# Two 3x3 convolutions whose halo operand holds a second, column-shifted copy of the halo rows: nine matmuls an image in place of twelve

## The chip, the cores and the metric

The kernel runs on one core of one Trainium2 chip. The metric is the device time of one execution in microseconds (us); the figure of a kernel is the median of its runs.

## What is computed

The input x has 8 images of 16 channels, 64 by 64 pixels. Four blocks follow one another, and each adds its result to x:

```python
x = x + L0(gn(x))   # a lattice of 16 cells, each a 3x3 convolution with bias and ReLU
x = x + L1(gn(x))   # one 3x3 convolution with circular borders, written in the reference with FFTs
x = x + L2(gn(x))   # a KAN convolution: 3x3 over SiLU and 8 spline features of each input
x = x + L3(gn(x))   # one 3x3 convolution with zero borders and a bias
```

gn is a group normalisation over 8 groups of channels of each image. Only L1 (the circular convolution) and L3 (the last convolution) are touched by the change.

## The kernel before

**Layout.** An image is held as 128 partitions by 16 wide rows of 33 columns (TS = 528 numbers, 512 of them pixels). The partition is (s, y, c): s is the parity of the column, y one of four interleaved row classes (row = 4q + y), c the channel. Each number is split into two parts, a rounded high part (written by ScalarE, ACT) and the remainder (written by VectorE, DVE), and a product of weight and image is three matmuls: high by high, high by low, low by high (`PRODUCTS`).

**One of the two convolutions, for one image** (`single_step`): all outputs need the rows of the own image at two column shifts (dx = 0 and 1: 2 x 3 matmuls of 128 x 128 by 512 columns). The outputs of row classes 0 and 3 also need the row class that lies in the next wide row above or below. Those rows are copied by DMA into a second operand, the halo: 64 rows (side, s, c), the other 64 rows of the operand being zero. It takes again two column shifts, 2 x 3 matmuls: twelve in all. The weights of the four cases stand in `W1` and `W3` as 4 tiles (own at two shifts, halo at two shifts) of two parts each; `single_spread` writes them by small DMAs from the POOL queue (24 for each convolution, in three steps of 8), and DVE clears rows 64 to 127 of the halo tiles of W1 at the start (`clear_weights`).

**Halo copies.** For L1, SP runs `l1_halos(j)` after all loads of the lattice: it waits until the low part of image j is there (`l1_lo`, line 778) and issues four DMAs from `circular_halos` (line 779). For L3, SP runs `l3_halos(b)` (lines 819 to 821): it waits for `l3_lo` and issues four DMAs from `image_halos`. TensorE (PE) waits in `l1_step` and `l3_step` for the low part and for all four DMAs of the image.

**The order around them.** In the last cell of the lattice PE runs, for b = 4 to 7, a cell step of 27 matmuls, small matmuls of means (`group_means`) and `l1_step(b - 4)`; then l1_step(4) to l1_step(7) follow, between them group means and `keep_warm` matmuls whose results nobody uses. Image j of L1 passes ACT (`l1_rows`), DVE (`l1_split_lo`), SP, the DMAs and PE in this order. The mean of image 3 for the KAN block (`group_means(1, 3)`) is queued on PE behind l1_step(5), and DVE's `tail(1, 3)` waits for it, with the whole of the first KAN features behind.

In the KAN block PE runs for each image b: 24 matmuls on the first four features (lines tagged 1696, as all of `products`), 30 matmuls of `halo_steps(b - 1)`, 6 on SiLU, from b = 3 the 12 of `l3_step(b - 3)`, and 24 on the other four features. SP runs for each image b: from b = 3 `l3_halos(b - 3)`, then 8 DMAs of the first features' halos (line 838; they wait until PE has read the halos of the image before), 4 for SiLU (line 835) and 8 for the other features. ACT may write the first features of the next image (line 1217) only after those 8 DMAs have landed; DVE writes their low part (line 1557), and PE's next image starts. After the last KAN image PE runs halo_steps(7), l3_step(5), group_means(2, 7), l3_step(6) and l3_step(7). The last image passes POOL (line 872), ACT (line 1229), DVE (line 1534), four halo DMAs (line 821), l3_step(7), DVE (line 1545) and the store.

## Time and profile before

| what | value |
|---|---|
| median of 3 runs | 1272.43 us (1270.22 to 1273.92) |
| span of the profiled execution, which is all that is known of its own time | 1275.4 us |
| mean granted TensorE clock over the span | 0.979 of full speed |
| busy share of PE, DVE, ACT, POOL | 93%, 60%, 53%, 30% |
| the lattice with L1's first images, to about | 1024 us |
| rest of L1 and the start of KAN, to about | 1098 us |
| KAN images 2 to 7 with L3's first images, to about | 1251 us |
| the last two images of L3 and the stores | to the end |

A time stamp is in us from the start of the span. The profile puts each wait down to the engine or DMA that released it. PE's clock has two levels here, 2.4 GHz (shown as 1.00) and 1.2 GHz (0.50); a mean between them is a stretch with both. An idle engine costs something only where the work that ends last waits for it.

### The profile page before, as it was taken

The numbers are of one execution on the slowest core, as the hardware profiler recorded it, in microseconds if no ns is written. First come the engines' busy times: TensorE is split into PE (matmuls) and PEld (weight loads), VectorE is DVE, ScalarE is ACT, GpSimd is POOL, SyncE is SP. The second block draws the span as 40 slices with busy tenths as digits, with TensorE's granted clock in tenths as the row PEclk, the third lists the DMA queues.
The fourth block names the chain that finished last, engine by engine and source line by source line (L and its number), as shares of the span: only waits on it lengthen the run. The fifth ranks groups of instructions, "written<-read, shape, count | busy, mean of one in ns | idle before, by whom it ended". The sixth has DMA issues, their size and how long they took to land.

```text
span 1275.4 us, 15041 instructions
## 1 busy us (share of the span) xinstructions
PE 1189.7 (93%) x5184; PEld 884.3 (69%) x5184; DVE 762.7 (60%) x967; ACT 675.0 (53%) x737; POOL 377.7 (30%) x544
## 2 busy tenths in 40 slices
PE   3888999999999999989999999998999987999995
PEld 2655677766666677766666677876777766777773
DVE  6798952455656522336554652226655789899952
ACT  1667854434544434444444543444434789789821
POOL 6221333235421012402113203633233542103212
PEclk9898999999999999999999999999999998999998
DMA  5899999999999967889989988988799414677773
GB/s 148 236 234 247 294 254 266 192 158 207 201 203 188 222 180 211 217 183 223 202 203 180 193 226 209 243 212 218 197 203 198 59 31 72 102 115 112 123 125 57
DMA packets 104687, 234.22 MB, mean 184 GB/s; under 512 B 36884, under 2 KB 49764, under 8 KB 96164
## 3 DMA queue, kind: packets, MB, share of 16 engines
q1 hardware_dynamic: 82624, 181.90, 66.1%
q0 software_dynamic: 15808, 24.31, 10.6%
q10 hardware_dynamic: 6180, 27.06, 6.7%
q8 instruction: 41, 0.67, 0.2%
q14 instruction: 34, 0.28, 0.1%
HBM read 124.15 MB, written 85.75 MB: 165 GB/s over the span
## 4 chain that ended last, share of the span: by engine, by line
PE 51%; SPq 19%; DVE 10%; DMA 10%; issue 5%; ACT 4%; POOL 0%; DVEq 0%; ACTq 0%; POOLq 0%
PE PB L1727 43%; SPq L807 15%; PE PB L1696 7%; DMA S<-lattice 4%; DMA lattice<-S 4%; SPq L786 2%; DMA F<-F 2%; ACT F L1141 2%; DVE S L1577 1%; DVE S L1564 1%; DVE S L1570 1%; DVE F L1557 1%; SPq L838 1%; PE PB L1687 1%; DVE F L1470 1%
## 5 line engine op out<-in xcount | busy, mean ns | idle before, releaser
L1727 PE MATMUL PB<-F,WA 128*96 128x512 f32 (+1 forms) x3792 | 916.9, 403 | 32.2 <-DVE F L1470 13.9
L1727 PEld LDWEIGHTS PB<-F,WA 128*96 128x96 f32 (+1 forms) x3792 | 662.7, 176 | 277.5 <-ACT F L1141 19.9
L1141 ACT ACTIVATE F<-S 128x2116 fp32r<-128x2116 f32 (+4 forms) x160 | 261.5, 1634 | 206.0 <-DMA S<-lattice 81.7
L1152 ACT ACTIVATE S<-PB,BIAS 96x512 f32<-96x512 f32 (+1 forms) x320 | 211.7, 683 | 294.5 <-PE PB L1727 292.3
L1458 DVE TENSOR_TENSOR F<-S,F 128x1089 fp32r<-128x1089 f32 (+2 forms) x80 | 121.4, 1518 | 184.2 <-ACT F L1141 183.3
L1460 DVE TENSOR_TENSOR F<-S,F 128x1058 fp32r<-128x1058 f32 x64 | 80.8, 1263 | 187.1 <-ACT F L1141 186.7
L1470 DVE CAST F<-F 64x528 fp32r<-64x528 f32 (+4 forms) x304 | 180.2, 642 | 3.5
L905 POOL DMA_DIRECT2D WA<-taps x76 | 56.5, 746 | 365.8 <-ACT S L1152 326.0
L1696 PE MATMUL PB<-F,WA 128*128 128x512 f32 x576 | 147.5, 414 | 14.0 <-DVE F L1557 14.0
L1696 PEld LDWEIGHTS PB<-F,WA 128*128 128x128 f32 x576 | 112.5, 197 | 43.3 <-issue 14.7
L1461 DVE TENSOR_TENSOR F<-S,F 64x1058 fp32r<-64x1058 f32 x64 | 82.1, 1282 | 0.0
L897 POOL DMA_DIRECT2D taps<-WX x112 | 68.2, 659 | 18.3 <-ACT S L1152 13.2
L872 POOL TENSOR_TENSOR RS<-VE,NHALF 128x1 f32<-128x1 f32 x25 | 27.9, 1115 | 121.0 <-DVE VE L1349 120.8
L890 POOL MEMSET WX<- 48x1600 f32 x18 | 26.3, 1461 | 108.8 <-ACT S L1152 84.4
L1464 DVE TENSOR_TENSOR F<-S,F 128x1089 fp32r<-128x1089 f32 x16 | 20.7, 1295 | 44.7 <-ACT F L1141 44.6
L1217 ACT ACTIVATE F<-S 128x2112 fp32r<-128x2112 f32 x16 | 31.4, 1964 | 23.3 <-DVE S L1577 12.2
L1190 ACT ACTIVATE S<-KS,CB 128x528 f32<-128x528 f32 x64 | 41.8, 725 | 0.2
L1557 DVE SCALAR_TENSOR_TENSOR F<-S,F 128x1056 fp32r<-128x1056 f32 x32 | 38.8, 1253 | 3.4 <-ACT F L1217 3.4
L1124 ACT ACTIVATE KAN<-X,NBI,RS 64x512 f32<-64x512 f32 (+1 forms) x48 | 32.5, 676 | 15.0 <-POOL F L1095 8.5
L1085 POOL DMA_DIRECT2D out<-OT x26 | 14.7, 574 | 83.1 <-DVE OT L1545 83.1
L1564 DVE SCALAR_TENSOR_TENSOR S<-S 128x2112 f32<-128x2112 f32 x16 | 37.7, 2354 | 2.3 <-ACT S L1201 2.3
L1577 DVE SCALAR_TENSOR_TENSOR S<-S 128x2112 f32<-128x2112 f32 x16 | 37.7, 2355 | 0.1
(130 smaller groups left out, 738.9 us busy)
## 6 DMA issues: line engine op xcount, KB each, us to landing
S<-lattice SPq DMA_DIRECT2D x448, 66.1 KB, 4.9
lattice<-S SPq DMA_DIRECT2D x32, 817.5 KB, 6.0
S<-lattice SPq DMA_DIRECT2D x160, 136.1 KB, 3.5
S<-lattice SPq DMA_DIRECT2D x72, 272.5 KB, 5.0
lattice<-S SPq DMA_DIRECT2D x52, 272.5 KB, 4.0
lattice<-S ACTq DMA_DIRECT2D x48, 272.5 KB, 4.7
lattice<-S ACTq DMA_DIRECT2D x16, 817.5 KB, 7.0
S<-lattice SPq DMA_DIRECT2D x160, 70.1 KB, 3.6
```

Source lines behind the costliest of these rows:

```text
L807: sp.dma_start(dst, src).then_inc(image_loaded[q], 16)
L897: pool.dma_start(dst, src).then_inc(tp_stored, 16)
L905: pool.dma_start(dst, src).then_inc(w_loaded[k % 2], 16)
L1141: act.activation(piece_view(s, h, 0), raw_view(s, h), ACT.Copy).then_inc(hi_ready, 1)
L1152: act.activation(wide(to[:, at:at + TS])[:, :, 0:RX], pixels(RING_BANK[n % SLOTS_O][0:cell.rows, :]), ACT.Relu, bias=BIAS[0:cell.rows, k:k ...
L1458: last = nc.vector.tensor_tensor(lo, raw, hi, ALU.subtract)
L1460: nc.vector.tensor_tensor(lo[:, 0:2], raw[:, 0:2], hi[:, 0:2], ALU.subtract)
L1461: last = nc.vector.tensor_tensor(lo[0:4 * C, 2:4], raw[0:4 * C, 2:4], hi[0:4 * C, 2:4], ALU.subtract)
L1470: last = nc.vector.tensor_copy(FP[4 * C:P, slot, part, to:to + n], FP[0:4 * C, slot, 0, source:source + n])
L1557: last = nc.vector.scalar_tensor_tensor(to[:, odd, :, 1], full[:, odd], 0.0, to[:, odd, :, 0].bitcast(F32), ALU.max, ALU.subtract)
L1696: last = nc.tensor.matmul(pixels(bank[:, :]), weights, moving, start=open_ and n == 0, stop=close and n == len(todo) - 1)
L1727: last = nc.tensor.matmul(bank, WA[0:rows, first:first + cell.rows], wide(FZ[0:rows, i % SLOTS_F, base:base + TS])[:, :, 0:RX], start=j == ...
```

## The change

`circular_halos` gets a parameter `shift`, and a new helper `shifted_halos` does the same for the last convolution: four further DMAs an image write the halo rows, moved by one column, into rows 64 to 127 of the halo operand. In L1 SP issues eight DMAs an image in place of four. In L3 SP issues eight for images 0 to 4; for images 5 to 7 SP issues four and ACT the four shifted ones, behind a new wait for `l3_lo(b + 1)` and ahead of the next image's `l3_rows`. The weights of the second halo shift go into rows 64 to 127 of halo tile 2 (`single_spread`: 32 DMAs for each convolution), tile 3 is no longer used, and the clear of W1's halo tiles goes. `single_step` does the halo with one shift, three matmuls for six. The waits of PE count eight DMAs an image.

```diff
--- before.py
+++ after.py
@@ -642,12 +642,18 @@
             for part in range(2):
                 src = WT[0:C, part, 0:720].bitcast(F32).rearrange("p (x f) -> p x f", x=5)
                 for s in range(2):
-                    blocks = [(s * 4 * C + y * C, 0, 4 - y) for y in range(4)]
-                    blocks += [(side * HALO + s * C, 2, (5, 0)[side]) for side in range(2)]
-                    for row, tile, first in blocks:
-                        dst = to[row:row + C, part, tile:tile + 2, :].bitcast(F32)
+                    for y in range(4):
+                        row, first = s * 4 * C + y * C, 4 - y
+                        dst = to[row:row + C, part, 0:2, :].bitcast(F32)
                         yield (dst.rearrange("p d (s f) -> p (d s) f", s=2),
                                src[:, s:s + 4, first * C:(first + 4) * C])
+                    for side in range(2):
+                        row, first = side * HALO + s * C, (5, 0)[side]
+                        for shift in range(2):
+                            dst = to[shift * 4 * C + row:shift * 4 * C + row + C, part, 2, :].bitcast(F32)
+                            x = s + 2 - 2 * shift
+                            yield (dst.rearrange("p (s f) -> p s f", s=2),
+                                   src[:, x:x + 2, first * C:(first + 4) * C])
 
         def own_tile(part, t, dx):
 
@@ -714,14 +720,27 @@
                 halo = halo_pair(g)[odd * 4 * C:(odd + 1) * 4 * C].rearrange("p t a f -> p (t a) f")
                 yield from image_halos(own, halo)
 
-        def circular_halos(z):
+        def circular_halos(z, shift):
 
             for side, y in enumerate((3, 0)):
                 for s in range(2):
                     rows = slice(s * 4 * C + y * C, s * 4 * C + (y + 1) * C)
-                    to = slice(side * HALO + s * C, side * HALO + (s + 1) * C)
-                    yield (F1[to, z, :, EXT:EXT + TS].bitcast(F32),
-                           F1[rows, z, :, 2 * RW * side:2 * RW * side + TS].bitcast(F32))
+                    first = shift * 4 * C + side * HALO + s * C
+                    at, n = 2 * RW * side + shift, TS - shift
+                    yield (F1[first:first + C, z, :, EXT:EXT + n].bitcast(F32),
+                           F1[rows, z, :, at:at + n].bitcast(F32))
+
+        def shifted_halos(own, halo):
+
+            for side, y in enumerate((3, 0)):
+                for s in range(2):
+                    src = own[s * 4 * C + y * C:s * 4 * C + (y + 1) * C].bitcast(F32)
+                    first = 4 * C + side * HALO + s * C
+                    dst = halo[first:first + C].bitcast(F32)
+                    if side == 0:
+                        yield dst[:, :, RW - 1:TS - 1], src[:, :, 0:TS - RW]
+                    else:
+                        yield dst[:, :, 0:TS - RW - 1], src[:, :, RW + 1:TS]
 
         def image_halos(own, halo):
 
@@ -775,8 +794,9 @@
 
                 z = j % SLOTS_1
                 sp.wait_ge(l1_lo, j + 1)
-                for dst, src in circular_halos(z):
-                    sp.dma_start(dst, src).then_inc(l1_halo[z], 16)
+                for shift in range(2):
+                    for dst, src in circular_halos(z, shift):
+                        sp.dma_start(dst, src).then_inc(l1_halo[z], 16)
 
             def store_outputs(s):
 
@@ -819,6 +839,9 @@
                 sp.wait_ge(l3_lo, b + 1)
                 for dst, src in image_halos(slot[:, 0], slot[:, 1]):
                     sp.dma_start(dst, src).then_inc(l3_halo[max(0, b - B + 3)], 16)
+                if b < B - 3:
+                    for dst, src in shifted_halos(slot[:, 0], slot[:, 1]):
+                        sp.dma_start(dst, src).then_inc(l3_halo[0], 16)
 
             for b in range(B):
                 if b >= 3:
@@ -1304,6 +1327,10 @@
                 if b == B - 2:
                     act.wait_ge(l3_clear, 2)
                 l3_rows(b)
+                slot = l3_slot(b)
+                act.wait_ge(l3_lo, b + 1)
+                for dst, src in shifted_halos(slot[:, 0], slot[:, 1]):
+                    act.dma_start(dst, src).then_inc(l3_halo[b - B + 3], 16)
 
 
         @block.vector
@@ -1319,7 +1346,6 @@
                 for first in (960, 2016, 2496, 2976):
                     nc.vector.memset(WA[4 * C:P, first:first + 96].bitcast(F32), 0.0)
                 nc.vector.memset(FZ[:, :, 2 * PIECE:FSLOT].bitcast(F32), 0.0)
-                nc.vector.memset(W1[4 * C:P, :, 2:4].bitcast(F32), 0.0)
                 nc.vector.memset(W3[:, :, :, :].bitcast(F32), 0.0).then_inc(wa_clear, 1)
 
             def turned_lo_part(name):
@@ -1733,15 +1759,13 @@
 
                 todo = [((weights[:, 0, 1 - dx], weights[:, 1, 1 - dx]), at_shift(own, P, dx)) for dx in range(2)]
                 products(bank, todo, True, False)
-                todo = [((weights[:, 0, 3 - dx], weights[:, 1, 3 - dx]), at_shift(halo, P, dx))
-                        for dx in range(2)]
-                return products(bank, todo, False, True)
+                return products(bank, [((weights[:, 0, 2], weights[:, 1, 2]), at_shift(halo, P, 0))], False, True)
 
             def l1_step(j):
 
                 z = j % SLOTS_1
                 pe.wait_ge(l1_lo, j + 1)
-                pe.wait_ge(l1_halo[z], 4 * 16 * (j // SLOTS_1 + 1))
+                pe.wait_ge(l1_halo[z], 8 * 16 * (j // SLOTS_1 + 1))
                 if j >= 2:
                     pe.wait_ge(added[1], j - 1)
                 single_step(OUT_BANK[j % 2], W1, F1_OWN[:, z], F1_HALO[:, z]).then_inc(l1_done, 1)
@@ -1813,7 +1837,7 @@
 
                 z = max(0, b - B + 3)
                 pe.wait_ge(l3_lo, b + 1)
-                pe.wait_ge(l3_halo[z], 4 * 16 * (b + 1 if z == 0 else 1))
+                pe.wait_ge(l3_halo[z], 8 * 16 * (b + 1 if z == 0 else 1))
                 if b >= 2:
                     pe.wait_ge(out_staged, b - 1)
                 single_step(LAST_BANK[b % 2], W3, l3_slot(b)[:, 0], l3_slot(b)[:, 1]).then_inc(l3_done, 1)
```

## Rows read from the trace of the kernel before

**Rows 1.** The page's chain that ended last: shares of the span by line

```profile
PE PB L1727 43%; SPq L807 15%; PE PB L1696 7%; DMA S<-lattice 4%; DMA lattice<-S 4%; SPq L786 2%; DMA F<-F 2%; ACT F L1141 2%; DVE S L1577 1%; DVE S L1564 1%; DVE S L1570 1%; DVE F L1557 1%; SPq L838 1%; PE PB L1687 1%; DVE F L1470 1%
```

**Rows 2.** Busy time by KAN image; columns: stretch, length, engines, clock, DMA share, GB/s

```profile
1171.05:1194.70 23.65, 23.21 (x99) 18.44 (x99) 23.37 (x23) 21.24 (x22) 6.68 (x6) 1.00 0.77 119
...
1218.35:1241.41 23.06, 23.06 (x98) 18.35 (x99) 11.83 (x18) 4.13 (x4) 3.00 (x6) 1.00 0.70 116
```

**Rows 3.** Groups by line and shape, PE; busy us, mean ns, idle before

```profile
L1696 PE MATMUL PB<-F,WX 128*128 128x512 f32 x96 | 26.1, 423 | 4.7 <-DMA F<-F 4.2 <-issue 0.5
...
L1696 PE MATMUL PB<-WA,W 128*128 128x512 f32 x72 | 18.0, 398 | 0.0
```

**Rows 4.** Chain of waits, 985 to 1100; columns: start us, us, what

```profile
991.98 5.91 DMA F<-F
...
998.02 3.09 PE PB L1696 x12
...
1025.66 0.58 SPq L779
...
1027.57 2.35 DMA F<-F
...
1030.17 4.49 PE PB L1696 x12
```

**Rows 5.** Timeline, 1034 to 1064; start us, us, engine, line, tiles, count, idle before

```profile
1034.98 0.16 DVE L1343 TENSOR_SCALAR GM<-PB 128x2 f32<-128x2 f32 x1 [1.59 <-PE PB L1647]
...
1062.90 8.60 PE L1696 MATMUL PB<-F,WA 128*128 128x512 f32 x24 [7.47 <-DVE F L1557]
```

**Rows 6.** Timeline of one KAN image, 1170 to 1205

```profile
1172.21 3.36 SPq L821 DMA_DIRECT2D WA<-WA  x4
...
1179.90 5.17 SPq L838 DMA_DIRECT2D F<-F  x8
...
1189.87 1.98 ACT L1217 ACTIVATE F<-S 128x2112 fp32r<-128x2112 f32 x1 [0.71 <-DMA F<-F]
...
1194.70 10.22 PE L1696 MATMUL PB<-F,WA 128*128 128x512 f32 x42 [0.44 <-DVE F L1557]
```

**Rows 7.** Timeline, the last images, 1245 to 1267

```profile
1245.79 3.03 PE L1696 MATMUL PB<-WX,WA 128*128 128x512 f32 x12
...
1248.65 2.99 PE L1696 MATMUL PB<-WA,W 128*128 128x512 f32 x12
...
1250.78 0.16 DVE L1337 SCALAR_TENSOR_TENSOR MV<-MV,NV 128x1 f32<-128x1 f32 x1
...
1251.49 0.28 PE L1647 MATMUL PB<-MV,G 128*128 128x2 f32 x2
...
1261.46 5.46 PE L1696 MATMUL PB<-F,W 128*128 128x512 f32 x12 [5.99 <-issue]
```

**Rows 8.** DMA engines: two short stretches, and issues of 1240.5 to 1241.25

```profile
990.00:992.00 2.00, 2.00 (x10) 1.57 (x9) 1.90 (x5) 1.99 (x3) 0.13 (x1) 1.00 1.09 59
...
1242.00:1244.00 2.00, 2.00 (x10) 1.60 (x9) 0.17 (x2) 0.00 (x0) 1.63 (x4) 1.00 1.09 149
...
WX<-F SPq DMA_DIRECT2D x2, 123.8 KB, 4.8
```

**Rows 9.** Start of the kernel, and the POOL queue at the weights of L3

```profile
21.75 0.48 DVE L1322 MEMSET WX<- 64x512 f32 x1
33.59 1.29 DVE L1458 TENSOR_TENSOR F<-S,F 64x1089 fp32r<-64x1089 f32 x1 [8.87 <-ACT F L1141]
...
L915 POOL DMA_DIRECT2D W<-WX x24: 514/514/682, 656.6 to 687.4; - x24
...
709.68 0.75 POOL L905 DMA_DIRECT2D WA<-taps  x1 [10.36 <-ACT S L1152]
```

**Rows 10.** Timeline of PE, two starts after idle time in the lattice

```profile
98.14 11.19 PE L1727 MATMUL PB<-F,WA 128*96 128x512 f32 x40 [1.82 <-ACT S L1152]
...
281.06 26.82 PE L1727 MATMUL PB<-F,WA 128*96 128x512 f32 x112 [1.10 <-ACT F L1141]
```


## The prediction

> **What bounds the kernel now.** The page's chain of waits comes first [rows 1]: most of what ends last is the lattice (its matmuls, line 1727, and SP's loads, line 807), which the change leaves alone. Products of line 1696, to which all 48 removed matmuls belong, hold 7%. So the question is not what 48 matmuls cost, but which of them end a wait. The groups by line give the price of one: 26.1 us for the 96 of L1 is 0.27 us, 18.0 us for 72 of L3 is 0.25 us (a mean duration of 400 ns overlaps the next one and is not the price) [rows 3]. If all 48 lay on the path, some 12 us would go.
>
> Three stretches decide. In L1 the chain runs through SP's halo DMAs: l1_step(0) starts when the fourth DMA has landed, and l1_step(5) too [rows 4]. What the reader is to see there is "DMA F<-F" right ahead of a matmul group: the operand is late, not PE. DVE in its turn sits idle for 1.59 us until the group means that PE has queued behind l1_step(5) [rows 5]. In the KAN block the busy times by image show PE at 23.21 and DVE at 23.37 of 23.65 us, so neither has much to give alone [rows 2]. The timeline shows a third loop of the same length: PE's halo steps free the halo tile, SP issues eight DMAs from 1179.90, ACT waits 0.71 us for their landing, and PE starts the next image at 1194.70 after an idle time of 0.44 us [rows 6]. From 1218.35 on PE alone fills the stretch, 23.06 of 23.06 us [rows 2], and from there to the end the last images pass from engine to engine [rows 7].
>
> **The sum** is made on the profiled execution, of which only the span of 1275.4 us is known; it is 3.0 us over the median of the runs, and I carry the difference over to the median, 1272.43.
>
> **L1, images 0 to 2.** The step between two of SP's issues is (1027.57 - 1025.66) / 3 = 0.64 us [rows 4], so four more end 2.55 us later. The eighth of image 0 would be issued at 991.98 + 2.55 = 994.5. How long it takes to land is not in the trace: 2.35 us as for image 5, or 5.91 us as for image 0 [rows 4], when the DMA engines were full (share 1.09 with only 59 GB/s [rows 8]). That is 996.9 to 1000.4. I take the middle, 998.7, since the load is on its way down by then: l1_step(0) starts 0.7 us later than its 998.02 (0 to +2.4). Nine matmuls for twelve give back 3 x 3.09 / 12 = 0.77 us in l1_step(0), (1) and (2), 2.3 us before image 5 is normalised behind the last cell. Halos 1 and 2 have a cell step of time and stay hidden; uncovered they would cost 2.55 us each. So image 5 is ready 1.6 us earlier (2.3 earlier to 0.1 later).
>
> **L1, image 5.** Its halo has no cover: +2.55 us. l1_step(5) starts at 1030.17 - 1.6 + 2.55 = 1031.1. Its 12 matmuls took 4.49 us, partly at half clock; after a longer idle time nine may all run at the 0.455 us of the last step (5.46 / 12 [rows 7]), 4.1 us. The saving is between 0.4 and 1.12 us (3/12 of 4.49); I take 0.4. Together **+0.55 us** at the wait of DVE [rows 5]. The good end is -2.3 + 2.55 - 1.12 = -0.9. At the bad end, 0.1 + 2.55 - 0.4 = +2.25, comes a clock that falls at l1_step(0): after 1.82 us idle 40 matmuls took 11.19 us, after 1.10 us idle 112 took 26.82 us, 0.280 against 0.239 us each, 1.6 us a fall [rows 10]; +3.9.
>
> **L1, image 7.** Its halo comes 2.55 us later too, hidden by PE's idle time of 7.47 us ahead of 1062.90 [rows 5]. 0; if that idle time got so short that the clock held, the 24 matmuls there could drop from 8.60 us towards 6.0: 0 to -2.6.
>
> **KAN images 3 to 6.** PE gets 0.75 us an image back, but the loops of DVE and of the halos stay, so its idle time grows from 0.44 to about 1.2 us and nothing ends sooner; DVE's own slack, 0.28 us an image, allows -1.1 in all. SP issues four more DMAs behind 1172.21: its 3.36 us become some 5.9, to 1178.1, ahead of 1179.90, when PE frees the tile [rows 6]. Hidden with 1.8 us to spare; without that cover the eight halo DMAs queued behind would start later, and ACT, DVE and PE with them. Traffic may still push their landing: 4 x 63 KB at 149 GB/s [rows 8] is 1.7 us of the DMA engines, of which I let up to 0.4 us an image show. **0** (-1.1 to +1.6).
>
> **From 1218 to the last means.** l3_step(4) lies on PE's path: -0.75. But PE's next twelve, at 1245.79, read halos of which the last were issued after 1240.5 and took 4.8 us [rows 7, 8]: they landed just in time, so at most 0.4 us is to be had. At the same time ACT would issue the four shifted DMAs of image 5 into full engines (share 1.09 [rows 8]); up to 1.7 us more for SP's. I take +0.7, under half of that, because those engines have gaps before. The DMA page of the Trainium skill (DMA: Bandwidth & Descriptors, "Issuing engines are not separate DMA queues") says that DMAs of all engines end up on the same 16 DMA engines and that a second issuing engine saves only issue time; taken at its word the whole 1.7 us would count, a sum higher by 1.0 us. Nothing in the trace of before has ACT and SP copying halos together. Behind these twelve, l3_step(5) gives up to 0.75 us back, but the mean that PE multiplies next is ready only at 1250.78 + 0.16, so group_means moves from 1251.49 by 0.55 at most [rows 7]. **+0.15** (-0.95 to +1.15).
>
> **The last image.** l3_step(7) runs at half clock: 3 x 0.455 = -1.37 us [rows 7]. The added wait of ACT for l3_lo holds up nothing of the last image; for image 6 the four issues stand ahead of ACT's l3_rows(7), which waits for the means anyway. Whether ACT's four DMAs land with SP's is unknown: 0 if they run side by side, +2.55 if one after the other; eight need 0.5 MB / 149 GB/s = 3.4 us instead of 2.5 for the issues, so +0.5, nearer to the first. **-0.9** (-1.4 to +1.2).
>
> **At nothing:** the clear of W1, 0.48 us of DVE, which then idles 8.87 us for the first loads; 16 more issues of POOL at 0.514 us, 8.2 us in six portions, where POOL idles 10.36 us in one wait [rows 9]. Uncovered they would delay a set of lattice weights by 1.6 us.
>
> Sum: 0.55 + 0 + 0 + 0.15 - 0.9 = -0.2 us, **1272.2 us**. About 0.3% (3.8 us) is what a measurement of this kernel can tell from no change.
>
> **Rivals.** (1) The halos stay hidden and PE's saving counts: -2.3 - 1.1 in L1, -0.75 - 0.55 from 1218 on, -1.37 at the end, -6.1: 1266.3. For it: from 1218.35 on PE is never idle [rows 2]. Against it: the DMA ahead of l1_step(0) and (5) [rows 4]. 0.14. (2) Slower: the late halos of L1 leave PE idle long enough for its clock to fall twice: +3.9 at l1_step(0) and (5) as above, and a second fall of 1.6 us in the matmuls after l1_step(5), on whose means DVE waits again, with -0.75 for the rest: +4.7, 1277.1. It decides where the idle time ahead of l1_step(0) becomes like the 1.82 us after which the 40 matmuls were slow [rows 10]. Against it: the landing may be short, and the first images give 2.3 us back. 0.14. (3) Slower, in the KAN block: PE's longer idle time, 1.2 us an image, lets the clock fall in images 3 to 6, 4 x 1.6 = +6.4: 1278.6. After 1.10 us idle the matmuls were fast, after 1.82 us some were not [rows 10], and 1.2 is near the first. 0.06. (4) ACT's four DMAs gain nothing over SP's queue: the last step +2.55 - 1.37, the halos at 1245.79 +1.7 - 0.55, L1 +0.55: +2.9, 1275.3. 0.12. [...]
>
> **Chances.** Forecast 0.54, all within 0.3%, as is (4). Faster 0.14, same 0.66, slower 0.20. The range leaves out (1) and (3), 0.20, and takes in the bounds of the forecast and (2): 1268.0 to 1277.5.
>
> **What would show it.** Right: eight issues of SP for each L1 image, 5.1 us long; l1_step(0) about 0.7 us later; DVE's wait for the means behind l1_step(5) longer by half a microsecond; KAN images at 23.6 us with PE idle for 1.2 us; the last step at some 4.1 us. Wrong: KAN images under 23.4 us, or l1_step(5) starting no later than before (the halos were not the limit); KAN images over 24 us with a clock under 1.00 (rival 3); the last step starting 2 us or more later after DVE's low part (rival 4).

## The result: 0.4% slower, and where the profile has it

The changed kernel takes 1278.83 us (median of 20 runs) against 1273.28 us for the kernel before (20 runs). The ratio is 1.0038 with a 95% interval of 1.0022 to 1.0054, which on 1274 us is +4.8 us (2.8 to 6.9). The forecast was 1272.2 us, no change; the time lies above its range. The profiled execution took 1282.15 us, with a span of 1280.4 us, against a span of 1275.4 us before.

The page's chain of the changed kernel again holds the lattice first [rows 1]. Lines have moved: the lattice is L1753 and L827, the products L1722, SP's halos of the KAN block L861.

```profile
PE PB L1753 51%; SPq L827 12%; PE PB L1722 5%; DMA F<-F 2%; DMA S<-lattice 2%; DVE S L1603 2%; DVE S L1590 2%; DVE S L1596 1%; SPq L861 1%; DVE F L1583 1%; DVE F L1484 1%; ACT F L1164 1%; DVE F L1496 1%; PE PB L1713 1%; DMA lattice<-S 1%
```

The products hold 5% for 7%. The groups of PE by line and shape (busy us, mean ns; idle time before them and what ended it) say what the matmuls gave and what came in their place:

```profile
L1722 PE MATMUL PB<-F,WX 128*128 128x512 f32 x72 | 23.4, 480 | 13.8 <-DMA F<-F 12.7 <-issue 1.1
...
L1722 PE MATMUL PB<-WA,W 128*128 128x512 f32 x54 | 14.1, 405 | 0.0
```

The answering group of before had 96 matmuls, 26.1 us busy, and waited 4.2 us for the halos [rows 3]. Now 72 matmuls are busy for 23.4 us, 0.33 us each instead of 0.27, and wait 12.7 us for the halos: 2.7 us of work saved, 8.5 us of waiting added. In L3's group (WA) the price per matmul hardly changes, 0.26 for 0.25 us.

**The unchanged lattice varies by more than the change is worth.** SP's first L1 halo issue, a point behind the unchanged matmuls of the lattice, comes between 980.1 and 994.1 us in the 13 traces of this study. A span of one trace therefore says little about a change of some microseconds. I compare stages instead, from these marks: *a*, SP's first L1 halo issue; the start of the first matmuls of l1_step(0) and l1_step(5); DVE's low part of the first features (128x1056) of images 4 and 7; the end of the span. The marks of the changed kernel, from the timelines of SP, PE and DVE (start, us, engine, line, tiles, idle time before):

```profile
988.57 11.55 SPq L799 DMA_DIRECT2D F<-F  x18
...
999.43 4.18 PE L1722 MATMUL PB<-F,WX 128*128 128x512 f32 x9 [4.14 <-DMA F<-F]
...
1034.79 4.18 PE L1722 MATMUL PB<-F,WX 128*128 128x512 f32 x9 [4.90 <-DMA F<-F]
...
1146.82 2.43 DVE L1583 SCALAR_TENSOR_TENSOR F<-S,F 128x1056 fp32r<-128x1056 f32 x2 [0.62 <-ACT F L1240]
...
1217.78 2.42 DVE L1583 SCALAR_TENSOR_TENSOR F<-S,F 128x1056 fp32r<-128x1056 f32 x2
```

The same marks of the kernel before (its l1_step(0) and l1_step(5) start at 998.02 and 1030.17 [rows 4]):

```profile
989.97 10.34 SPq L779 DMA_DIRECT2D F<-F  x9
...
1144.82 2.43 DVE L1557 SCALAR_TENSOR_TENSOR F<-S,F 128x1056 fp32r<-128x1056 f32 x2 [0.66 <-ACT F L1217]
...
1215.78 2.42 DVE L1557 SCALAR_TENSOR_TENSOR F<-S,F 128x1056 fp32r<-128x1056 f32 x2
```

So in the changed kernel image 4's mark is 1146.82 - 988.57 = 158.25 us behind a, the stretch from image 4 to 7 is 70.96 us, and the tail 1280.4 - 1217.78 = 62.62 us. The same differences in all traces (matmuls an image / halo DMAs an image; "split" is explained below, and there "halo" is the start of the matmuls on the halo; in e6 and e11 the trace shows the own part of l1_step(5) in one row with l1_step(4)):

| kernel | a | l1_step(0) | l1_step(5) | image 4 | image 4 to 7 | tail |
|---|---|---|---|---|---|---|
| before, 12/4 | 989.97 | +8.05 | +40.20 | +154.85 | 70.96 | 59.62 |
| after, 9/8 | 988.57 | +10.86 | +46.22 | +158.25 | 70.96 | 62.62 |
| e8, after again | 990.60 | +9.91 | +45.28 | +157.36 | 70.96 | 62.28 |
| e1, 12/8 | 986.67 | +8.33 | +43.07 | +156.74 | 70.94 | 62.75 |
| e2, 9/4 | 980.12 | +6.51 | +36.68 | +150.75 | 70.94 | 57.89 |
| e3, L1 9/8, L3 12/4 | 990.26 | +7.90 | +40.65 | +154.29 | 70.95 | 59.70 |
| e4, L1 12/4, L3 9/8 | 990.83 | +6.54 | +38.62 | +151.81 | 70.94 | 60.82 |
| e7, 9/8, image 5 by SP | 989.94 | +9.22 | +41.98 | +156.39 | 70.96 | 59.71 |
| e10, 9/8, more keep_warm | 994.08 | +8.81 | +41.48 | +155.47 | 70.96 | 61.09 |
| e6, 12/4 split | 985.77 | +6.54 | halo +38.60 | +152.08 | 70.94 | 57.11 |
| e11, e6 again | 992.09 | +6.52 | halo +38.39 | +151.93 | 70.96 | 57.32 |
| e5, 9/8 split | 986.28 | +6.52 | own +33.60, halo +39.27 | +148.80 | 70.96 | 60.16 |
| e9, 9/8 split, image 5 by SP | 991.33 | +6.55 | halo +41.29 | +153.28 | 70.95 | 55.94 |

Between before and after, the lattice is 1.4 us shorter, L1 3.4 us longer, images 4 to 7 equal, the tail 3.0 us longer; together the 5.0 us of the spans. L1's stage varies by 3 to 4 us between traces of equal L1 code (154.85 and 151.81 with 12/4; 158.25, 157.36, 154.29 and 156.39 with 9/8). The means of these, 153.3 and 156.6, differ by 3.2 us, no more than such traces differ among themselves. The tail with L3 as before is 59.62 and 59.70 us, with the change 62.62, 62.28, 60.82 and 61.09 us, on average 2.0 us more. 3.2 + 2.0 = 5.2 us stands beside the measured 4.8.

**L1.** PE's timeline around l1_step(0) and the step behind it, then l1_step(4), (5), (7) and the second features, and DVE's wait for the means:

```profile
1003.40 5.25 PE L1753 MATMUL PB<-F,WA 128*128 128x512 f32 x18
...
1027.51 2.38 PE L1722 MATMUL PB<-F,WX 128*128 128x512 f32 x9 [1.12 <-issue]
...
1039.30 0.16 DVE L1369 TENSOR_SCALAR GM<-PB 128x2 f32<-128x2 f32 x1 [3.85 <-PE PB L1673]
...
1051.81 3.20 PE L1722 MATMUL PB<-F,WX 128*128 128x512 f32 x9 [3.62 <-DMA F<-F]
...
1067.19 7.25 PE L1722 MATMUL PB<-F,WA 128*128 128x512 f32 x24 [4.15 <-DVE F L1583]
```

l1_step(0) waits 4.14 us for its eight copies, and its nine matmuls then take 4.18 us (row of 999.43, above) where nine take 2.38 us at 1027.51: the engine came back from its wait at a lower clock. The windows (length; busy us and count of PE, weight loads, DVE, ACT, POOL; granted clock, DMA share, GB/s) show it, and the DMA engines still at a share of 0.89 while it waits:

```profile
998.00:1000.00 2.00, 0.57 (x2) 0.51 (x3) 1.59 (x2) 0.35 (x1) 0.83 (x2) 0.60 0.89 159
...
1004.00:1006.00 2.00, 2.00 (x8) 1.57 (x7) 1.52 (x5) 0.00 (x0) 0.00 (x0) 0.69 0.44 71
```

The clock is at 0.60 and 0.69 here, between the two levels, and at 0.50 in the 4 us between; the 18 matmuls of the cell step behind take 5.25 us (4.42 us in kernels whose clock held). l1_step(5) pays the same again, 4.90 us of waiting and 4.18 us of work, and DVE, which waited 1.59 us for the means behind it [rows 5], waits 3.85 us. l1_step(7) waits 3.62 us where it waited 0.45 us before; the wait ahead of the second features covers that.

**The tail.** The timelines of SP, ACT and PE:

```profile
1237.24 6.17 SPq L861 DMA_DIRECT2D WX<-F  x8
...
1238.52 3.57 ACTq L1333 DMA_DIRECT2D WA<-WA  x4
...
1249.52 4.35 PE L1722 MATMUL PB<-WX,WA 128*128 128x512 f32 x12 [2.27 <-DMA WX<-F]
...
1253.67 2.63 PE L1722 MATMUL PB<-WA,W 128*128 128x512 f32 x9
...
1267.71 4.05 PE L1722 MATMUL PB<-F,W 128*128 128x512 f32 x9 [8.96 <-DMA F<-F]
```

ACT issues its four copies for image 5 in the midst of the eight by which SP brings the halos of the last KAN image. The last of SP's eight lands 7.1 us after its issue, against 4.8 us [rows 8]:

```profile
WX<-F SPq DMA_DIRECT2D x1, 123.8 KB, 7.1
```

PE, which read those halos without a gap before [rows 7], waits 2.27 us and comes back at a lower clock (granted 0.75 and 0.50 in the two stretches of 2 us from 1250 on): twelve matmuls in 4.35 us for 3.03. From there everything up to the last step is late. The timeline of DVE has the update of image 7 (from PB to X) and the low part of the last image (F); first the kernel before, then the changed one:

```profile
1248.86 0.75 DVE L1525 SCALAR_TENSOR_TENSOR X<-PB,OB,X 128x512 f32<-128x512 f32 x1 [0.83 <-PE PB L1696]
...
1255.72 0.71 DVE L1534 TENSOR_TENSOR F<-KAN,F 128x528 fp32r<-128x528 f32 x1 [1.85 <-ACT F L1229]
```

```profile
1253.91 0.75 DVE L1551 SCALAR_TENSOR_TENSOR X<-PB,OB,X 128x512 f32<-128x512 f32 x1 [4.59 <-PE PB L1722]
...
1260.44 0.71 DVE L1560 TENSOR_TENSOR F<-KAN,F 128x528 fp32r<-128x528 f32 x1 [1.85 <-ACT F L1252]
```

Measured from image 7's mark, the update moves from +33.08 to +36.13 us and the last step from +45.68 to +49.93; only then come back 1.41 us, since the last step's nine matmuls take 4.05 us for 5.46.

### The profile page after: what moved, and what is told of

Read it like the earlier page. It is cut to its first block, busy times and chain, and to the rows that moved or that the text cites. A ratio compares the mean times of both kernels' runs of the same rounds, so it can differ in the third digit from the quotient of the medians.

```text
span 1280.4 us, 15024 instructions
## 1 busy us (share of the span) xinstructions
PE 1179.8 (92%) x5136; PEld 875.6 (68%) x5136; DVE 761.3 (59%) x966; ACT 675.7 (53%) x737; POOL 389.8 (30%) x560
## 4 chain that ended last, share of the span: by engine, by line
PE 58%; SPq 16%; DVE 11%; DMA 5%; issue 5%; ACT 3%; POOL 1%; ACTq 0%; DVEq 0%; POOLq 0%
PE PB L1753 51%; SPq L827 12%; PE PB L1722 5%; DMA F<-F 2%; DMA S<-lattice 2%; DVE S L1603 2%; DVE S L1590 2%; DVE S L1596 1%; SPq L861 1%; DVE F L1583 1%; DVE F L1484 1%; ACT F L1164 1%; DVE F L1496 1%; PE PB L1713 1%; DMA lattice<-S 1%
## 5 line engine op out<-in xcount | busy, mean ns | idle before, releaser
L1753 PE MATMUL PB<-F,WA 128*96 128x512 f32 (+1 forms) x3792 | 916.7, 403 | 31.9 <-DVE F L1496 19.4
L1753 PEld LDWEIGHTS PB<-F,WA 128*96 128x96 f32 (+1 forms) x3792 | 662.4, 176 | 277.6 <-issue 24.0
L1722 PE MATMUL PB<-F,WA 128*128 128x512 f32 x576 | 145.2, 409 | 14.0 <-DVE F L1583 14.0
L1722 PEld LDWEIGHTS PB<-F,WA 128*128 128x128 f32 x576 | 110.8, 194 | 43.0 <-issue 15.2
```

The lines of the kernel that those rows point to most:

```text
L1722: last = nc.tensor.matmul(pixels(bank[:, :]), weights, moving, start=open_ and n == 0, stop=close and n == len(todo) - 1)
L1753: last = nc.tensor.matmul(bank, WA[0:rows, first:first + cell.rows], wide(FZ[0:rows, i % SLOTS_F, base:base + TS])[:, :, 0:RX], start=j == ...
```

## The experiments

**Theory A**: the added copies make the halos land later, PE waits for them in L1 and at the end, and its clock falls in these waits; the saved matmuls are worth what rival (1) of the prediction gave them. **Theory B**: the time comes from elsewhere, from the lattice, whose POOL queue issues 16 more DMAs. Within A, the tail has a question of its own: whether it is the number of copies or that ACT issues some of them among SP's. Ratios are against the kernel before, run on the same chip beside it, from 12 runs of the kernel tried; us are the ratio on 1274.

**e1: the eight copies with the old twelve matmuls.** In the changed kernel:

```diff
-                return products(bank, [((weights[:, 0, 2], weights[:, 1, 2]), at_shift(halo, P, 0))], False, True)
+                todo = [((weights[:, 0, 3 - dx], weights[:, 1, 3 - dx]), at_shift(halo, P, dx)) for dx in range(2)]
+                return products(bank, todo, False, True)
```

with the weights spread and cleared as before, so that rows 64 to 127 of the halo meet zero weights.

> Before's twelve matmuls and weights, with the eight halo DMAs an image of the changed kernel (the shifted copies land on rows whose weights are zero). Theory A, the loss is the four further DMAs (later landing in L1, a clock that falls there, ACT's copies among SP's at the end): slower than before by 8 to 12 us, since nothing is saved; l1_step(0) about 10.9 us after SP's first halo issue, as in the changed kernel, for 8.0 before. Theory B, the loss comes from the lattice (the weights' further POOL issues, the order of its DMAs), and what L1 shows differs from run to run: within 3 us of before.

Ratio 1.0069 (1.0045 to 1.0093): +8.8 us (5.7 to 11.8). So the copies cost all of the loss and more. The trace, of the fastest of the 12 runs, has less of it: +1.9 us in L1 and +3.1 us in the tail against before's. And not all came as Theory A had it: l1_step(0) starts 8.33 us after a and not 10.9, and there and at the twelve matmuls of the tail the clock held, after waits of 1.64 and 1.12 us. So copies cost time without a fall of the clock at these points too.

**e2: the nine matmuls with four copies.** All issues of `shifted_halos` and of `circular_halos(z, 1)` go, PE waits for four, and the clear of W1's halo tiles stays:

```diff
-                for shift in range(2):
-                    for dst, src in circular_halos(z, shift):
-                        sp.dma_start(dst, src).then_inc(l1_halo[z], 16)
+                for dst, src in circular_halos(z):
+                    sp.dma_start(dst, src).then_inc(l1_halo[z], 16)
```

> Nine matmuls and the new weights, but no shifted copies (four DMAs an image as before): one column's share of the halo rows is left out of both convolutions. Theory A: faster than before by 4 to 7 us (my rival 1 had 6.1). Theory B: slower by 3 to 5 us, as the changed kernel, since the POOL issues are all there.

Ratio 0.9950 (0.9923 to 0.9977): -6.4 us (-9.8 to -2.9). This kernel keeps all of POOL's added issues and is faster than before, so Theory B falls. PE's timeline at l1_step(0), l1_step(5) and the last step:

```profile
986.63 2.30 PE L1702 MATMUL PB<-F,WX 128*128 128x512 f32 x9
...
1016.80 3.89 PE L1702 MATMUL PB<-F,WX 128*128 128x512 f32 x9 [3.62 <-DMA F<-F]
...
1247.01 4.18 PE L1702 MATMUL PB<-F,W 128*128 128x512 f32 x9 [6.95 <-issue]
```

With four copies l1_step(0) doesn't wait at all in this trace (1.34 us in before's). What the change removes is worth 6.4 us, what it adds costs 8.8 us, and 8.8 - 6.4 = 2.4 us, uncertain by about 4.6 us with these two intervals, agrees with the measured 4.8.

**e3 and e4: one convolution at a time.** e3 keeps the change in L1 and gives L3 its old weights, four copies and twelve matmuls; e4 the other way round (of the edits, PE's call alone is shown):

```diff
 # e3
-                single_step(LAST_BANK[b % 2], W3, l3_slot(b)[:, 0], l3_slot(b)[:, 1]).then_inc(l3_done, 1)
+                single_step_old(LAST_BANK[b % 2], W3, l3_slot(b)[:, 0], l3_slot(b)[:, 1]).then_inc(l3_done, 1)
 # e4
-                single_step(OUT_BANK[j % 2], W1, F1_OWN[:, z], F1_HALO[:, z]).then_inc(l1_done, 1)
+                single_step_old(OUT_BANK[j % 2], W1, F1_OWN[:, z], F1_HALO[:, z]).then_inc(l1_done, 1)
```

> The change in L1 alone. Theory A: +5.7 us in L1, of which 2.3 us come back before KAN image 3 because PE's clock is higher there, as in the two profiles: +3.4 us (2 to 5), the tail as before. Theory B: about half of the whole loss, +2.5 us, with no difference between the first L1 halo and the KAN block.

> The change in L3 alone. Theory A: KAN images at 23.6 us as before; from the matmuls on the last halos to the end +2.8 us, of which the last step gives nothing back (1.4 us fewer matmuls, 1.5 us later halos): +2 to +3 us. Theory B: the other half, +2.5 us, with no difference after 1218 us.

e3: 1.0014 (0.9984 to 1.0043), +1.8 us; e4: 1.0015 (0.9989 to 1.0041), +1.9 us. Neither alone is told from no change; their sum, 3.7 us, agrees with the whole. e3 lost a little less than the 2 to 5 us expected. In the stage table the tail follows its edit: 59.70 us in e3, as before, and 60.82 in e4. L1 does so less clearly: 154.29 us in e3 is 2.5 us above e4's 151.81 and 0.6 below before's. In both traces the clock held at a point where it fell in the changed kernel. e3 at l1_step(0) (PE's timeline):

```profile
998.16 2.37 PE L1731 MATMUL PB<-F,WX 128*128 128x512 f32 x9 [1.21 <-DMA F<-F]
```

e4 at the twelve matmuls of the tail:

```profile
1244.61 3.13 PE L1739 MATMUL PB<-WX,WA 128*128 128x512 f32 x12 [1.56 <-DMA WX<-F]
```

The waits were 1.21 and 1.56 us here, 4.14 and 2.27 us in the changed kernel's trace, so the same edit does not cost the same in every trace.

**e7: the tail's culprit.** SP issues the shifted copies of image 5, behind the KAN halos, in place of ACT:

```diff
-                if b < B - 3:
+                if b < B - 2:
                     for dst, src in shifted_halos(slot[:, 0], slot[:, 1]):
-                        sp.dma_start(dst, src).then_inc(l3_halo[0], 16)
+                        sp.dma_start(dst, src).then_inc(l3_halo[max(0, b - B + 3)], 16)
```

and ACT's four wait and go out only for b >= B - 2.

> The changed kernel, with the four shifted copies of L3's image 5 issued by SP behind KAN's last halos, not by ACT in the midst of them. Theory A: PE no longer waits for KAN's last halos (2.3 us in the changed kernel's trace): faster than the changed kernel by 1.5 to 2.3 us, slower than before by 2.5 to 3.4 us. If the copies cost by their number and not by their place: no difference from the changed kernel (+4.9 us).

Ratio 1.0038 (1.0011 to 1.0064), beside 1.0053 (1.0030 to 1.0076) for the changed kernel run again beside it (e8). These intervals overlap, and the first 20 runs of the changed kernel had 1.0038 too; but run side by side the medians are 1279.07 and 1282.18 us, and the means of the 12 runs each differ by 3.2 us (95% interval 0.5 to 6.0), near the 1.5 to 2.3 us expected. In the trace the cause is plain, PE's timeline at the same twelve matmuls of e7:

```profile
1247.02 3.09 PE L1723 MATMUL PB<-WX,WA 128*128 128x512 f32 x12 [0.26 <-DMA WX<-F]
```

and of e8:

```profile
1250.59 4.30 PE L1722 MATMUL PB<-WX,WA 128*128 128x512 f32 x12 [2.20 <-DMA WX<-F]
```

The wait shrinks from 2.20 to 0.26 us, the clock holds, and the tail is 59.71 us, 2.6 us below e8's. The number of copies is the same; what counts is that ACT's stood among SP's. All traces agree: PE waits for these halos for 1.12 to 2.33 us in the six that have ACT's copies in SP's burst (the changed kernel, e1, e4, e5, e8, e10) and for at most 0.27 us in the other seven.

e8 is the changed kernel itself; it was run to stand beside e7:

> The changed kernel once more, beside the others on one chip and with a second trace: +3 to +7 us against before. Theory A has l1_step(0) start 7.9 to 10.9 us after SP's first halo issue (with four DMAs 6.5 to 8.1), and the stretch from the low part of KAN image 7's first features to the end at 62 to 63 us (59.6 before).

Its +6.8 us (3.8 to 9.7) include the first measurement's 4.8. Its trace repeats the first one: the wait and the fall at l1_step(0) (3.22 us, 4.18 us for nine matmuls) and at the twelve matmuls just shown.

**e10: the clock at l1_step(0) kept up by more idle work.**

```diff
-                        keep_warm(PB[1], 10)
+                        keep_warm(PB[1], 20)
```

> The changed kernel with 20 unused matmuls for 10 ahead of l1_step(0), so that PE's idle time there falls from 3 to 4 us to 1 to 2 us. If the fallen clock is what makes L1 dear: l1_step(0) at 2.4 us for 4.2, the cell step behind it at 4.4 for 5.3, in all 2 to 3 us faster than the changed kernel, 2 to 3 us slower than before. If it is the late copies alone: l1_step(0) starts as late and DVE's features are as late: no difference from the changed kernel.

The added matmuls cover the wait for the halos, and the nine matmuls of l1_step(0) take 2.31 us (PE's timeline):

```profile
1002.89 2.31 PE L1722 MATMUL PB<-F,WX 128*128 128x512 f32 x9
```

The ratio is 1.0037 (1.0017 to 1.0058), that of the changed kernel itself. That is what the late copies alone would give, but 2 to 3 us slower than before, the other expectation, is inside the interval too: inconclusive. L1's stage is 155.47 us in this trace, inside the spread of the others, so how much of L1's 3 us the first fall of the clock makes up was not measured.

**e5, e6, e9, e11: the halo wait moved inside the step.** If late halos are the cost, PE should not wait for them before its six products on the own image, which don't need them. The same edit in the changed kernel (e5) and in the kernel before (e6, with four for eight; e11 is e6 run again), for L1 and L3 alike:

```diff
-            def single_step(bank, weights, own, halo):
+            def single_step(bank, weights, own, halo, landed):
...
                 products(bank, todo, True, False)
+                pe.wait_ge(*landed)
...
-                pe.wait_ge(l1_halo[z], 8 * 16 * (j // SLOTS_1 + 1))
-                single_step(OUT_BANK[j % 2], W1, F1_OWN[:, z], F1_HALO[:, z]).then_inc(l1_done, 1)
+                single_step(OUT_BANK[j % 2], W1, F1_OWN[:, z], F1_HALO[:, z],
+                            (l1_halo[z], 8 * 16 * (j // SLOTS_1 + 1))).then_inc(l1_done, 1)
```

e9 is e5 together with e7.

> The changed kernel, with PE's wait for the halos moved behind the six matmuls on the own rows. Theory A (the halos are late, and PE's idle time costs clock): of each late step six matmuls run while the halos land; 1.5 to 4 us less than the changed kernel in L1 and 2.7 us (6 x 0.455) less at the last step, the waiting matmuls on KAN's last halos as in the changed kernel: between 4 us faster and 1 us slower than before. Theory C, the cost is the load on the DMA engines ahead of the KAN halos and in L1's first image, whatever PE does meanwhile: only the 2.7 us of the last step come back, some 2 us slower than before.

> The kernel before with the same move of the wait and nothing else: twelve matmuls, four DMAs. Theory A: faster than before by 3 to 6 us (2.7 us at the last step, some 2 us at l1_step(5), up to 1 us at l1_step(0)), so more than all that the change could save. If PE's matmuls in these steps were the limit and not the halos: no difference.

> The changed kernel with both repairs: PE waits for the halos behind the own matmuls, and SP issues the shifted copies of image 5. Theory A (the losses are the waits on late copies): the sum of the two effects, 4 to 7 us faster than before, near the split kernel with twelve matmuls, since the fewer matmuls save 0.7 us in L1 and the last step's three are paid back by its later halos. Rival D (the nine matmuls are worth their 6 us once the waits are hidden): 8 to 11 us faster than before, clearly ahead of the split kernel with twelve.

> The split kernel with twelve matmuls and four copies once more, beside the split kernel with nine: 3 to 7 us faster than before; the difference to the other split kernel shows what the packed halo is worth when its waits are hidden (theory A: under 2 us, rival D: 3 us or more).

| kernel | ratio | 95% interval | us |
|---|---|---|---|
| e5, 9/8 split | 0.9993 | 0.9965 to 1.0020 | -0.9 |
| e6, 12/4 split | 0.9958 | 0.9931 to 0.9984 | -5.4 |
| e11, e6 again | 0.9968 | 0.9949 to 0.9987 | -4.1 |
| e9, 9/8 split, image 5 by SP | 0.9951 | 0.9928 to 0.9974 | -6.2 |

The split takes the change's loss away (e5: beside e8, run with it, the mean of its 12 runs is 8.8 us lower, 95% interval 5.7 to 11.9), and without the change it is a gain (e6, e11). Theory C's +2 us for e5 is still inside the interval against before (up to +2.5); against it stands L1's stage of 148.80 us, the shortest of all, where C would leave it as long as the changed kernel's. Image 5's two parts and the last step in e6, PE's timeline:

```profile
1018.59 4.52 PE L1696 MATMUL PB<-F,WX 128*128 128x512 f32 x18
...
1024.37 1.69 PE L1696 MATMUL PB<-F,WX 128*128 128x512 f32 x6 [1.25 <-DMA F<-F]
...
1249.46 2.53 PE L1696 MATMUL PB<-F,W 128*128 128x512 f32 x6 [1.75 <-DVE F L1534]
...
1254.41 2.93 PE L1696 MATMUL PB<-F,W 128*128 128x512 f32 x6 [2.42 <-DMA F<-F]
```

The first row holds l1_step(4) and the own part of l1_step(5); the wait before the halo part is 1.25 us, and the six matmuls take 1.69 us at full clock. In e5 the same wait is 4.02 us, and the last step's halo part waits 3.55 us:

```profile
1025.55 1.65 PE L1722 MATMUL PB<-F,WX 128*128 128x512 f32 x3 [4.02 <-DMA F<-F]
...
1237.84 4.45 PE L1722 MATMUL PB<-WX,WA 128*128 128x512 f32 x12 [2.33 <-DMA WX<-F]
...
1249.63 2.93 PE L1722 MATMUL PB<-F,W 128*128 128x512 f32 x6 [2.48 <-DVE F L1560]
...
1256.11 1.58 PE L1722 MATMUL PB<-F,W 128*128 128x512 f32 x3 [3.55 <-DMA F<-F]
```

At the end, the halo part starts 1256.11 - 1249.63 = 6.48 us behind the own part in e5 and 1254.41 - 1249.46 = 4.95 us behind it in e6. Those 1.5 us are what eight copies cost there, and they use up what the three saved matmuls give (2.93 against 1.58 us). The row of 1237.84 also shows that the split leaves the tail's other loss, ACT's copies in SP's burst, where it was; e9 takes that away too. e9 and e11, run side by side, have medians of 1268.09 and 1269.50 us; the means differ by 1.0 us, with a 95% interval from 4.1 us faster to 2.0 us slower for e9. L1 and tail together are equal in their traces, 153.28 + 55.94 and 151.93 + 57.32 us. So with the wait split, packing the halos has nothing left to give that these runs can see; rival D's 3 us are not excluded by the times, and its 8 to 11 us against before only just (e9's interval ends at 9.2).

## Why the prediction was wrong, point by point

**L1, images 0 to 2: the failed step.** "So image 5 is ready 1.6 us earlier" is the sentence that failed. The last piece of DVE's low part of image 5 starts 3.5 us later against a in the changed kernel (1026.99 - 988.57 = 38.42 us) than before (1024.93 - 989.97 = 34.96), and 2.5 us later in e8. DVE's timeline, the kernel before and then the changed one:

```profile
1024.93 0.70 DVE L1481 TENSOR_TENSOR F<-KAN,F 128x528 fp32r<-128x528 f32 x1
```

```profile
1026.99 0.71 DVE L1507 TENSOR_TENSOR F<-KAN,F 128x528 fp32r<-128x528 f32 x1
```

Two of its terms were mis-sized. First, l1_step(0) starts 2.8 us later against a than before, 1.9 us in e8, where +0.7 (0 to 2.4) was forecast. The added copies of image 0 were given a landing in the middle between 2.35 and 5.91 us. Over all of L1 the copies from SP's line land in 2.3 us at the least, 2.4 in the median and 6.3 at the most:

```profile
DMA to landing us min/median/max: 2.3/2.4/6.3
```

The first ones are the slow ones: the four added copies of image 0 take 5.5 us here (median). Second, the sum had no price for the clock, which stood only in the bad end of the term and in rival (2): 1.8 us in the nine matmuls (4.18 for 2.38) and 0.8 us in the 18 behind them (5.25 for 4.42), 2.6 us where the bound had 1.6. The 2.3 us that the fewer matmuls should give back in three steps are 2.1 us (3 x 0.71).

The sentence does not fail in every execution. With the same code in L1, image 5 is ready 0.8 us earlier than before in e7 and 2.1 us earlier in e3, where l1_step(0) starts 1.2 us later and 0.2 us earlier, the four copies take 4.3 and 2.9 us and the clock holds at this point. So the forecast's middle is among the cases that occur; that one trace of before could stand for all of them was the tacit premise, and e4's, with the same L1 code, has image 5 ready 1.6 us earlier than before's.

**L1, image 5: right.** "Its halo has no cover: +2.55 us": from that low part to l1_step(5) it takes 5.24 to 5.28 us in the three traces with four copies and no split (before, e4, e2) and 7.78 to 7.80 us in the six with eight (the changed kernel, e1, e3, e7, e8, e10). The duration of its nine matmuls, forecast 4.1 us, is 4.18 us. l1_step(5) so starts 6.0 us later against a in the changed kernel's trace, 5.1 us in e8, 1.8 in e7 and 0.4 in e3, where 0.9 was forecast. DVE's wait grew by 2.26 us, not 0.55, and the whole term for L1 is about +3 us, inside the bounds given for it (-0.9 to +3.9) but far from the value taken. Rival (2) had the mechanism: it put L1 at +5.5 us (3.9 + 1.6), with a second fall in the matmuls behind l1_step(5), which did not come: the 24 `keep_warm` matmuls there take 5.88 us in e8, 0.245 us each, near the 0.239 us of the fast stretch [rows 10]. That its total of +4.7 us is so near the measured +4.8 is luck: it had too much in L1 and a gain of 0.75 us for the rest, where there was a loss.

Of the 6.0 us at l1_step(5), 3.4 arrive at image 4's first features (the column "image 4" of the table). Where the other 2.6 are made up was not followed step by step. PE's second features, forecast to absorb a later image 7, do so: their idle time shrinks from 7.47 to 4.15 us, and their 24 matmuls take 7.25 us for 8.60.

**KAN images: right.** The period of image 5's stretch is 23.65 us with eight copies too, and PE's idle time before the first features is 1.17 us, forecast 1.2:

```profile
1173.05:1196.70 23.65, 22.49 (x96) 17.86 (x96) 23.37 (x23) 21.21 (x22) 6.68 (x6) 1.00 0.81 130
...
1173.05 10.22 PE L1722 MATMUL PB<-F,WA 128*128 128x512 f32 x42 [1.17 <-DVE F L1583]
...
1181.88 5.60 SPq L861 DMA_DIRECT2D F<-F  x8
...
1191.85 1.97 ACT L1240 ACTIVATE F<-S 128x2112 fp32r<-128x2112 f32 x1 [1.42 <-DMA F<-F]
```

PE is 0.72 us less busy and idle for as much longer [rows 2, 6]; the clock stays at 1.00, which rejects rival (3). ACT's wait for the halos doubled, 1.42 for 0.71 us, the traffic that was allowed for, and DVE at 23.37 of 23.65 us hid it. 70.94 to 70.96 us for three images in all 13 traces is the cleanest number of this study: in this block neither copies nor matmuls of the change count.

**From 1218 to the last means: mis-sized.** +0.15 was forecast, the good share -0.55 against +0.7 for ACT's four copies. The update of image 7 came 3.05 us later (36.13 for 33.08). The step that failed is "I take +0.7, under half of that, because those engines have gaps before". The twelve matmuls are the last of a chain that "landed just in time", as the prediction itself said, so a later landing is paid whole, and after PE's wait of 2.27 us its matmuls ran 1.3 us longer at the lower clock (4.35 for 3.03), which the term didn't hold at all; the saved matmuls gave a little back. The rest of the term was sound: in e7, without ACT's copies in the burst, the update comes 0.2 us earlier than before. With them it comes 1.1 to 1.6 us later where the clock held (e1, e4, e10) and 2.9 to 3.1 us later where it fell (e8, the changed kernel). The sentence of the Trainium skill that was weighed there (DMA: Bandwidth & Descriptors, "Issuing engines are not separate DMA queues") is borne out by e7: the copies of ACT push SP's, on the same engines, and the landing of 7.1 us for 4.8 is 2.3 us more in this trace, above the 1.7 us that were worked out from the traffic alone.

**The last image: direction wrong, half of the reason right.** Its matmuls save 1.41 us (forecast 1.37). But the step starts 1.53 us later behind its own DVE part (49.93 - 42.66 = 7.27 us for 45.68 - 39.94 = 5.74) where +0.5 was taken: ACT's and SP's four copies neither run freely side by side (0) nor one after the other (+2.55); it is +1.4 to +1.8 us in all six traces with eight copies and no split. The term is +0.1, not -0.9. Rival (4) had its "2 us or more" nearly, and its sum of +2.9 us held L1 at +0.55.

**At nothing, right as far as it was tried:** POOL's issues (e2 keeps all of them and is faster), and the wait that ACT got (from the update of image 7 to the last low part it takes 6.53 us, 6.86 before). What the clear of W1, which went, was worth was not tried by itself.

**The price of the matmuls was right, that of the copies not.** Rival (1) gave the matmuls 6.1 us; e2 measures 6.4 (2.9 to 9.8). The sum of -0.2 us thus set 5.9 us against them for the copies. e1 measures 8.8 (5.7 to 11.8) with twelve matmuls; with nine, the changed kernel against e2, it is 4.8 + 6.4 = 11.2 us, uncertain by some 4. The clock is a part of what is missing: each longer wait of PE was costed as a wait, and the matmuls behind it as if they ran at the old speed, outside of one bound. In the changed kernel's trace that part is 2.6 us in L1 and 1.3 us in the tail. How large it is in the medians is not shown: e1 is slow although the clock held at both points in its trace, and e10, which kept it up at l1_step(0), is not measurably faster than the changed kernel.

**Open.** Why l1_step(0) starts 6.5 us after a in some traces and 10.9 in others was not tried; the copies themselves and POOL's loads of the KAN weights at the same time are both possible. The added copies can't be all of it: e3 and e8 have the same L1 code and differ by 2.0 us at l1_step(0), and with four copies it starts 8.05 us after a in before and 6.54 in e4.

## What to carry to other kernels

A DMA that replaces a matmul has to be late nowhere: first ask of each copy who waits for its landing, and where PE waits longer, add a price for a fall of the clock behind the wait, which was 1.3 to 2.6 us in the changed kernel's trace, though it did not come in every trace. Before a second engine issues copies, see what the first one's queue is moving at that moment. And where a step needs two operands of which one comes late, put the wait between its two halves: that alone took 4 to 5 us off the kernel before, and left the packing nothing that these runs can measure.

## What the runs showed of the hardware that was not expected

**The same idle time, two clocks.** Ahead of l1_step(4) PE is idle for 1.12 to 1.16 us in five traces. In the changed kernel and e8 its nine matmuls then take 2.38 us (row of 1027.51 above); in e3, e7 and e10, after 1.14, 1.16 and 1.16 us, they take 3.88, 3.55 and 3.78 us. This is e3:

```profile
1023.66 3.88 PE L1731 MATMUL PB<-F,WX 128*128 128x512 f32 x9 [1.14 <-issue]
```

And in e7 l1_step(0) runs at full speed after 2.50 us of idle time, when twelve matmuls in the changed kernel's tail did not after 2.27:

```profile
999.16 2.38 PE L1723 MATMUL PB<-F,WX 128*128 128x512 f32 x9 [2.50 <-DMA F<-F]
```

So the length of one idle time does not settle it. The two kernels that were fast at l1_step(4) are those whose clock had fallen at l1_step(0); that this is the reason was not tried.

**Issues are slower in a full burst, but not whenever two engines issue.** ACT's four copies of image 5 take 3.45 to 4.56 us to issue in the six traces in which they stand among SP's eight of 124 KB (3.57 in the changed kernel's). Its four of images 6 and 7, with four by SP starting within 0.1 us of them, take 2.54 and 2.78 us in the changed kernel. SP's own eight take 5.80 to 6.93 us with ACT's copies among them and 5.29 to 6.57 us without, so that ACT's issues slow SP's is not shown.
